# Two-layer recurrence and mixture-of-experts kernel: the one-hots of the early routing divided between GpSimd and VectorE, 72 columns wide, in other steps of the recurrence

## The reference

```
def step(h, z_t):
    gate = jax.nn.sigmoid(h @ Wh.T + z_t @ Wz.T + b)
    h_new = jnp.tanh(h * leak + gate * z_t)
...
gate_hidden = jnp.einsum('nh,erh->ner', x, W_A)
scores = jnp.sqrt(jnp.sum(gate_hidden * gate_hidden, axis=-1))
topk_scores, topk_idx = jax.lax.top_k(scores, K)
...
g = jnp.einsum('ner,efr->nef', gate_hidden, W_B)
up = jnp.einsum('nh,efh->nef', x, W_up)
y = jnp.einsum('nef,ehf->neh', jax.nn.silu(g) * up, W_down)
out = jnp.einsum('neh,ne->nh', y, w_full)
```

## Time and profile before

| | |
|---|---|
| runs | 390.03, 392.41, 393.56 us (median 392.41) |
| profiled execution | 392.09 us, of which the span in the trace is 390.1 us |
| mean granted TensorE clock | 0.952 |
| busy share of the span | PE 84%, VectorE 70%, ScalarE 60%, GpSimd 55% |
| recurrence of layer 0 | scans from 10.9 to 123.4 us |
| crossing to steady expert tiles | 123.4 to about 142 us |
| expert tiles | to about 285 us, then layer 1 |

### The profile page before, as it was taken

The page is one execution under the profiler, slowest core; times in us unless marked ns, Lnnn a source line. Parts: engine busy times, 40 slices in busy tenths (PEclk is TensorE's granted clock), DMA queues, the critical chain, the costliest instruction groups (busy, mean ns, idle before and its releaser), DMA issues.

```text
span 390.1 us, 11984 instructions
## 1 busy us (share of the span) xinstructions
PE 327.8 (84%) x3816; PEld 231.3 (59%) x3817; DVE 272.2 (70%) x922; ACT 232.7 (60%) x733; POOL 214.0 (55%) x203
## 2 busy tenths in 40 slices
PE   2687777777577789999999999999987999999962
PEld 1444444444353357767777777777675777877841
DVE  5545555567996279587597878544456999999870
ACT  2356656565446446565656565565545878777871
POOL 5659999999804354454444745653115555562220
PEclk9999999998965699999999999999996999999998
DMA  8992185461592133222323332334213122221001
GB/s 209 201 396 103 42 297 188 160 244 64 193 337 75 29 124 89 66 86 68 90 64 91 90 89 73 96 82 79 69 39 97 32 83 69 81 67 41 29 29 40
DMA packets 22536, 42.95 MB, mean 110 GB/s; under 512 B 3986, under 2 KB 14610, under 8 KB 21604
## 3 DMA queue, kind: packets, MB, share of 16 engines
q0 software_dynamic: 6560, 23.17, 19.7%
q1 hardware_dynamic: 15664, 19.31, 15.7%
q10 hardware_dynamic: 276, 0.01, 0.0%
HBM read 28.97 MB, written 13.50 MB: 109 GB/s over the span
## 4 chain that ended last, share of the span: by engine, by line
PE 46%; DVE 14%; ACT 5%; issue 3%; DMA 2%; POOLq 0%; DVEq 0%; POOL 0%; ACTq 0%
PE bank L996 13%; PE bank L972 13%; PE bank L959 4%; PE bank L984 4%; DVE peak L1638 2%; PE bank L950 2%; DVE wrec L1599 2%; DVE h_lo L1669 1%; PE bank L952 1%; PE bank L1094 1%; PE bank L788 1%; PE bank L795 1%; DVE z_lo L1659 1%; PE bank L1111 1%; ACT z_hi L706 1%
## 5 line engine op out<-in xcount | busy, mean ns | idle before, releaser
L497 POOL DMA_INDIRECT xs<-hs_rows,row_of_slot x39 | 37.0, 948 | 72.3 <-PE bank L952 55.7
L788 PE MATMUL bank<-h_hi,wrec_hi 128*128 128x32 f16 x512 | 43.7, 181 | 29.3 <-ACT h_hi L595 27.8
L788 PEld LDWEIGHTS bank<-h_hi,wrec_hi 128*128 128x128 f16 x512 | 34.3, 97 | 56.0 <-ACT h_hi L595 49.6
L972 PE MATMUL bank<-wup_s,xt 128*128 x234 | 64.4, 385 | 0.0
L996 PE MATMUL bank<-wdn_s,wrec 128*128 x468 | 57.8, 273 | 0.3 <-ACT wrec L641 0.3
L996 PEld LDWEIGHTS bank<-wdn_s,wrec 128*128 128x128 f16 x468 | 45.2, 98 | 14.6 <-issue 1.1
L1492 DVE TENSOR_TENSOR wrec<-bank,wrec 128x512 f16<-128x512 f32 x39 | 27.0, 691 | 35.2 <-ACT wrec L641 34.8
L519 POOL DMA_INDIRECT z_lo<-y_rows,slot_i x32 | 31.1, 970 | 27.5 <-issue 26.4
L500 POOL DMA_INDIRECT gs<-gate_rows,row_of_slot x39 | 37.4, 958 | 11.9 <-issue 11.6
L1231 DVE TENSOR_TENSOR_SCAN bank<-bank,terms 128x128 f32<-128x128 f32 x64 | 27.6, 431 | 22.5 <-ACT bank L591 20.6
L788 PE MATMUL bank<-h_hi,wrec_lo 128*128 128x32 f16 x512 | 42.2, 178 | 0.0
(11 more groups left out here) (245 smaller groups left out, 964.1 us busy)
## 6 DMA issues: line engine op xcount, KB each, us to landing
y_rows<-z_lo SPq DMA_DIRECT2D x39, 128.0 KB, 1.8
stage<-wup POOLq DMA_DIRECT2D x2, 2048.0 KB, 10.8
gate_rows<-ga_s SPq DMA_DIRECT2D x16, 256.0 KB, 3.0
stage<-wdn POOLq DMA_DIRECT2D x2, 2048.0 KB, 10.5
stage<-wb SPq DMA_DIRECT2D x2, 1024.0 KB, 14.0
hs_rows<-hs_out SPq DMA_DIRECT2D x16, 128.0 KB, 2.3
stage<-w POOLq DMA_DIRECT2D x2, 1024.0 KB, 7.5
stage<-x_tm POOLq DMA_DIRECT2D x1, 2048.0 KB, 15.0
```

The lines of the kernel that those rows point to most:

```text
L497: pool.indirect_dma_start(out=xs[par][:, :], out_offset=None, in_=hs_dram[0:tokens, :], in_offset=bass.IndirectOffsetOnAxis(ap=row_of_slot ...
L788: mm(fm(par)[:, ft, cols], w[:, m, kt, fcols], h_hi[pp][:, kt, pcols], start=False, stop=True, skip_group_check=True)
L972: ins = mm(bank[4 + par][:, :], xt[par][:, b, kt, :], w_slice(wup_s, a, kt, e), start=kt == 0 and n == 0, stop=kt == KT - 1 and n == 2)
```

## The change

1. The one-hots of c = 1 move from VectorE to GpSimd (nine pairs, in front of the three loads). GpSimd reads its columns from `iota_slot` in SBUF. A new semaphore, s_places, tells it that columns and rows are ready, and hot_pool counts what it has made.
2. VectorE makes the nine pairs of c = 0, in other steps. The column one-hot is 72 wide (EARLY_COLS = 8 * 9) for both engines, and so are the products and the copy that read it.
3. The links of the chain move to earlier steps: `loads` from (12, 1) to (12, 0), `times_rank` and `ranks_early` to (12, 1), `places_early` and `place_of` to (12, 2), the products to (13, 3), (14, 0), (14, 1) and (14, 2), the copy of the inverse from (15, 0) to (14, 2), `list_of` and `list_rows` from (15, 0) and (15, 1) to (14, 3).
4. GpSimd's split of two layer-1 matrices (m = 2, 3) moves from in front of the gathers to behind the gathers of slot tiles 1 and 2.
5. In the crossing, TensorE transposes slot tile 0 in front of the gates of tile 15. ScalarE copies it in before the gates of tile 14, and loads the Silu table later. VectorE forms silu times up of slot tile 0, and the low gates of slot tiles 1 and 2, in front of the last scores and of the late picks.

```diff
@@ gpsimd
+            pool.wait_ge(s_places, 1)
+            for t in range(EARLY):
+                pool.tensor_scalar(early[0][:, 1, t, 0:EARLY_COLS], iota_slot[:, 0:EARLY_COLS], col_of[:, 1, t:t + 1], None,
+                                   ALU.is_equal)
+                pool.tensor_scalar(early[1][:, 1, t, :], iota_slot[:, :], row_in[:, 1, t:t + 1], token_id[:, t:t + 1],
+                                   ALU.is_equal, ALU.mult).then_inc(hot_pool, 1)
+
             pool.dma_start(stage[0][:, 0:KT * HID].rearrange("p (k n) -> p k n", k=KT),
...
-            for m in (2, 3):
+
+            def split_rec(m):
...
             for j in range(FIRST):
                 gather_h(j, j % 2, EARLY * P)
+                if j in (1, 2):
+                    split_rec(j + 1)
@@ scalar
-            sc.activation(warm[:, 1:2], c_round[:, :], ACT.Silu)
...
             copy_in(0, 0)
+            copy_gates(TILES - 2, 0)
+            sc.activation(warm[:, 1:2], c_round[:, :], ACT.Silu)
+            silu_of(0, 0)
+            copy_in(1, 1)
             sc.wait_ge(gate_mm, TILES)
@@ tensor
-            def inverse_early(first, end):
+            def inverse_early(pairs):
                 pe.wait_ge(sel_ready[0], 1)
...
+                for c, t in pairs:
+                    pe.wait_ge((hot_ready[0], hot_pool)[c], t + 1)
+                    ins = mm(bank[6][0:EARLY_COLS, 256:384], early[0][:, c, t, 0:EARLY_COLS], early[1][:, c, t, :],
...
+            transposed_in(0, 0)
+            pe.wait_ge(hi_ready, STEPS)
+            gates_of(TILES - 1, 1, 0, 4)
+            pe.wait_ge(lo_ready, STEPS)
+            gates_of(TILES - 1, 1, 4, 6)
+            rows_of(TILES - 1, 1)
             pe.wait_ge(s_wts, 1)
-            transposed_in(0, 0)
@@ vector
+            hot_after_terms = {(12, 2): 0, (12, 3): 1, (13, 1): 2, (13, 2): 4, (13, 3): 6, (14, 1): 8}
+            hot_after_scan = {(13, 2): 3, (13, 3): 5, (14, 1): 7}
...
+            gates_low(0, 0)
+            sum_squares(TILES - 2, 0)
+            sum_squares(TILES - 2, 1)
+            expert_tile(0, 0, gates_low_ahead=1)
             sum_squares(TILES - 1, 0)
             sum_squares(TILES - 1, 1)
-            gates_low(1, 1)
             dve.wait_ge(score_done, 2 * TILES)
             pick_late(0)
-
-            expert_tile(0, 0)
             pick_late(1)
```

More of the change, by code:

```diff
@@ L31 @@
 COLS = E * CAP
+EARLY_COLS = E * EARLY
 BIG = 3.0e38
@@ L877, in place_of @@
                 mm(bank[b][:, 129:130], before[:, :], avail[:, c:c + 1], start=True, stop=True).then_inc(place_mm[c], 1)
-            def inverse(b, hots, first, end, n):
-                for m in range(first, end):
-                    ins = mm(bank[b][:, 256:384], hots[0][:, m % 2, m // 2, :], hots[1][:, m % 2, m // 2, :],
-                             start=m == 0, stop=m == n - 1)
-                return ins
-            def inverse_early(first, end):
-                pe.wait_ge(sel_ready[0], 1)
-                pe.wait_ge(hot_ready[0], end)
-                ins = inverse(6, early, first, end, 2 * EARLY)
-                if end == 2 * EARLY:
+            def inverse_early(pairs):
+                pe.wait_ge(sel_ready[0], 1)
+                for c, t in pairs:
+                    pe.wait_ge((hot_ready[0], hot_pool)[c], t + 1)
+                    ins = mm(bank[6][0:EARLY_COLS, 256:384], early[0][:, c, t, 0:EARLY_COLS], early[1][:, c, t, :],
+                             start=(c, t) == (0, 0), stop=(c, t) == (0, EARLY - 1))
+                if (c, t) == (0, EARLY - 1):
                     ins.then_inc(inv_mm[0], 1)
@@ L895, in inverse_late @@
                 pe.wait_ge(hot_ready[1], n)
-                inverse(1, late, 0, n, n).then_inc(inv_mm[1], 1)
+                for m in range(n):
+                    ins = mm(bank[1][:, 256:384], late[0][:, m % 2, m // 2, :], late[1][:, m % 2, m // 2, :],
+                             start=m == 0, stop=m == n - 1)
+                ins.then_inc(inv_mm[1], 1)
             def list_of(c, b):
@@ L1232, in gate_tile @@
                                           ALU.mult, ALU.add).then_inc(v_ready, 1)
-                    if live(k - 3) and s == 0:
+                    if live(k - 3) and s == 0 and not moved(k):
                         sum_squares(k - 3, 0)
@@ L1524, in _ @@
             expert_tile(2, 0)
-            hots(1, 0, 6)
+            hots_late(0, 6)
             expert_tile(3, 1)
             place_tiles(1, 1)
-            hots(1, 6, 11)
+            hots_late(6, 11)
             expert_tile(4, 0)
-            hots(1, 11, 2 * late_n)
+            hots_late(11, 2 * late_n)
             expert_tile(5, 1)
```

89 lines of the change are left out of this document (46 added, 43 removed).

## The result

The changed kernel takes 394.03 us (median of 20 runs, 392.47 to 395.82); the kernel before took 390.4 us beside it (median of 20 runs, 389.67 to 393.56; the first three of them had given 392.41). The ratio is 1.0076, with a 95% interval of 1.0056 to 1.0095. So the kernel became 0.8% slower, where 388.8 us and a small gain were predicted; 394.03 lies above the range. The profiled execution took 393.25 us (span 391.3) against 392.09 (span 390.1).

The account below looks back on a forecast made before the run. The recurrence bounds up to 123 us, then the crossing to 142, then TensorE. The recurrence's 5.3 us gain is lost waiting for the gather; first `down` comes 3.4 us earlier: 392.09 - 3.4 = 388.7, forecast 388.8, range 384.8 to 393.6.

Parts of the forecast that it names:

- the price of GpSimd's pairs: One-hots on GpSimd before the loads: 0.55 us a pair, nine pairs 5.0 us, first load issued at 105.4.
- The queue: GpSimd's DMA queue: loads finish at 122.1, the gather of slot tile 0 waits behind them and lands at 122.6.
- the crossing: From landing at 122.6 to first `down` at 138.5: gate product 126.8, transposes of slot tile 1 end at 129.6.
- The recurrence: Steps with one-hots fall to 1.66 to 1.70 us; 5.3 us gained, last scan at 118.1 instead of 123.4.
- the load of the word: In the crossing, loading the word of the experts, now open: between 0 and 1.5 us, taken as 0.5.
- The sum: Whole kernel: profiled execution 392.09 less 3.4 gives 388.7 us; 388.8 forecast, 0.9% under 392.41.
- (c): Rival: GpSimd's one-hots are dear; gain gone at 0.93 us a pair, 393.7 us at 1.1; chance 0.17.

Follow-up runs that it names:

- e5: The kernel before with fourteen one-instruction probes in GpSimd's idle time, varying width, operation, scalars and input; 413.09 us against 412.98 (one run).
- e1: The changed kernel with the three loads issued ahead of GpSimd's nine pairs of one-hots; 415.92 us, ratio 0.9993 to the kernel before.
- e2: The changed kernel with the three loads issued from SyncE's queue instead of GpSimd's; 413.11 us, ratio 0.9953 to the kernel before.
- e10: The same kernel as e8, run once more on another chip; 407.35 us, ratio 0.9828 to the kernel before.
- e4: The kernel before with the new order of the crossing alone; 415.28 us, ratio 1.0006 to the kernel before.
- e7: The changed kernel with the three loads behind the fourth pair of one-hots instead of the ninth; 412.75 us, ratio 1.0000 to the kernel before.
- e11: e8 with SyncE's load of x_tm moved behind the last store of gates; 409.64 us, ratio 0.9929 to the kernel before.
- e6: The changed kernel itself, run on a second chip; 414.43 us, ratio 1.0051 to the kernel before.
- e8: The changed kernel with pairs before GpSimd's last subtraction, loads from SyncE, act_low of slot tile 0 between the late picks; 407.83 us, ratio 0.9871 to before.

## Why the prediction was wrong, point by point

The step that failed is the price of GpSimd's pairs, 0.55 us in the prediction and 1.21 us in the trace. The queue and the crossing held, and the part of the recurrence that came out too good did so by the same price.

**The recurrence: mechanism right, 1.25 us too good.** The steps with one-hots are 1.66 us, as predicted. (12, 1) cost nothing: the scan of (12, 2) is at 95.55, where I had put 96.2. The last scan is at 119.35 and not 118.1, because of the 1.8 us that TensorE waits for pairs in (14, 2). That wait stood in the text with its condition ("at 1.0 us a pair it would begin to"), and the condition was met.

**GpSimd's pairs: the step that failed.** "I take 0.55, since the rows nearest in kind give it and since the fixed part overlaps if anything." The rows were of mult and add without a compare; they priced that right (0.30 us, e5), but the one-hot is a compare, and that costs 0.35 us more, the pointers 0.15. I had even bounded it at 1.1 us a pair from above, and the truth, 1.21 us, lies beyond that bound. Nine pairs took 10.9 us instead of 5.0; they began 0.5 us earlier than I took, and so the first load was issued at 110.82 instead of 105.4.

The Trainium skill ("GPSIMD Engine Reference", key points) puts elementwise work on GpSimd at about twice VectorE's time. Here the pair takes 1.21 us on GpSimd and took 0.58 on VectorE, a factor of 2.1; the widths and the input differ, though. Like for like, the one-hot of 128 columns from SBUF with two pointers is 0.79 us to VectorE's 0.33, a factor of 2.4. I had set the rule behind the rows, since splits didn't show it; for the compare it was nearer than they were.

**The queue: right.** From the first load's issue to the gather's landing I had 17.2 us, and it was 114.12 + 13.51 - 110.82 = 16.8. The wait of TensorE for it is 8.18 us. e1 and e2 show that the loads cause it.

By the Trainium skill ("DMA: Bandwidth & Descriptors", section on queues, rings and completion order) the descriptors of a ring are consumed in ring order, and an engine takes turns only between rings. The traces agree: in the changed kernel the gather took 13.51 us in the queue of the loads and landed at 127.63, behind x_tm, which was issued at 112.52 and landed 14.8 us later, at 127.3. With the load in another queue, in e10, x_tm was issued at 114.10 and landed 10.7 us later, at 124.8, while the gather issued after it, at 115.01, landed at 122.07, ahead of it.

**The crossing: right, and in its parts too.** From the start of the transposes to the end of the first `down` it is 143.32 - 127.68 = 15.6 us, where the sum had 15.9. To the gate product it is 131.49 - 127.68 = 3.8 us (4.15 predicted): the load of the word cost nothing on the chain, where I had 0.5. From there to the end of the transposes of slot tile 1, at 134.17 + 0.13, it is 2.8 us, as predicted. The granted clock is 0.50 up to 132 us and 0.79 from 132 to 134, so it came back at about 132.8 us (an estimate from that mean), during `up`. From the end of those transposes to the end of the first `down` it is 9.0 us (8.9 predicted). act_low stands directly behind the picks (141.83, then 141.97), and `down` waits 1.67 us for it.

**The sum.** The rival (c), "the gain is 3.4 - 9 * (p - 0.55)", gives with p = 1.21 a loss of 2.5 us, 394.6 in the profiled execution. The profiled execution took 393.25: the pairs began 0.5 us earlier than I took, the landing was 0.4 us quicker and the crossing 0.3. So (c) is what happened, and it had 0.17, of which 0.08 for more than 1%. The chance was too small, since an operation that no row shows was priced at its lower bound. Against the median of the kernel before, 390.4, the loss is 3.6 us and not 1.2: the profiled execution from which the sum starts was 1.7 us over that median, which three runs could not tell.

**What stays open.** On the other chips two things appear that the first chip's traces don't have, and I found the cause of neither.

The first is a long step (15, 1). It takes 1.84 us in the changed kernel's trace on the first chip and 2.85 to 3.71 us in each of the nine traces of kernels with the new routing on the other chips; e4 and e5, with the old routing, have 1.83. In the chain of e1 it stands as a stretch in which nothing that the profile shows is waited for:

```profile
120.81 2.09 issue
```

Where TensorE doesn't wait for a gather behind it (e1, e2, e7, e11) it delays the crossing by 1 to 2 us.

The second lies between the end of the first `down` and the end of the last. That is 145.2 us in both kernels on the first chip, and 154.5 us (e4, e7) to 159.4 (e11) on the others, with 157.7 in e5, 154.8 in e6, 155.6 in e8 and 156.6 in e10. Many slot tiles have the first chip's pitch of 3.8 us there too; others take 4.1 to 4.5 us and a few 5.7 to 8.3. In e6 ScalarE stands idle for 2.89, 2.31 and 3.84 us in front of three instructions (at 231.14, 262.68 and 269.17), without a releaser that the profile names, and TensorE waits for ScalarE behind two of them; the traces of the first chip have no such rows. They add up to 9.0 us, where the whole stretch is 9.6 us longer. As it varies by some us from trace to trace, a gain at 140 us and a gain in the median can differ by as much. Against e5's 139.48 the first `down` is 3.8 us later in e6 and 5.8 us earlier in e8; their medians are 1.5 us over and 5.2 us under that of the kernel before.

## What to carry to other kernels

Price an operation that is moved to another engine by a row of the same operation there; if there is none, leave its price wide open in the forecast. Here a row of another operation gave less than half, and even the upper bound, twice that, was too low. When work is put in front of DMA issues, follow the queue to the transfer that is wanted first: here nine pairs of small instructions cost the recurrence 1.8 us directly, but through the loads behind them they cost TensorE a wait of 8.2 us for one gather. Put what is wanted early in front of long work that is wanted late (the pairs before the last subtraction), and long loads into a queue with no gather behind them; beside such a load a gather was still slow (7.1 us).

## What the runs showed of the hardware

- GpSimd, 128 columns: mult and add 0.30 us, is_equal and mult 0.65 us with immediates and 0.79 us with two pointers; 2.5 to 3.4 ns a column where a compare is in it (e5). VectorE makes the same one-hot from SBUF in 0.33 us (128 columns, two pointers, the mean of 14 in e2's late routing).
- A gather of 128 rows lands 2.7 to 3.4 us behind its issue in a quiet queue (the kernel before), 13.5 us behind it with 4 MB of loads in front in its own queue (the changed kernel), and 7.0 to 7.1 us behind it beside a 2 MB load in another (e8, e10, e11).
- The granted clock of a stretch is not a property of the kernel alone. The kernel before has 0.50 (108 to 113 us), 0.84 (113 to 118) and 0.50 (123.5 to 133, in the crossing) in its own trace; e5, whose TensorE work is the same, has 1.00, 1.00 and 0.75 there on another chip. The first `down` ends at 141.93 in the one and 139.48 in the other.
